# Head 2's loads and products, the q statistics and the engine orders in a convolution-attention and FFN kernel

## The chip, the cores and the metric

The kernel runs on one core of one Trainium2 chip. The metric is the device time of one execution in microseconds (us). TensorE is called PE (PEld: its weight loads), VectorE DVE, ScalarE ACT, GpSimd POOL and SyncE SP, as in the profile.

## The reference, cut to what matters

```python
def xattn(k, v, q, ssm_kernel, D, head_dim):      # k = v = ctx_2048, q = layernorm(x); (8, 128, 256)
    kv = jnp.einsum('bhil,bhjl->bijhl', k_, v_)    # 16 heads of 8 rows: all products of two rows
    y = causal convolution of kv with ssm_kernel[h] along l (by FFT of 2 * 256)
    out = y + kv * D[h]
    return jnp.einsum('bijhl,bhil->bjhl', out, q_)
def ffn(x):                                        # integer weights less 128, times a scale per row
    return down(silu(gate(x)) * up(x))             # 256 -> 704 -> 256
x = x + xattn(ctx_2048, ctx_2048, layernorm(x), ssm_kernel, D, 8)
x = x + ffn(layernorm(x))
```

All is float32. The layer norms have no weights.

## The kernel before

**Attention.** Positions (256, in two halves of 128) lie on partitions, and the work goes head by head, 16 heads. For each head `products[n]` holds the products of two of the eight context rows for all eight batches: since k = v only those with a distance of 0 to 4 rows are made, 288 columns a half are convolved. Two instructions make them: the squares (ACT, `squares(n)`) and the four other distances (POOL, `pairs(n)`); for heads 0 and 1 DVE makes all five distances at once (`all_products`, one call for each half; `DVE_MADE = 2`). The convolution is three multiplications by parts of a Toeplitz matrix of the head's taps, each run as two PE instructions: `convolve_across(n)` (first half into second) and `convolve_within(n)` (each half into itself). The Toeplitz matrices come by DMA with shifted rows, those of heads 0 to 7 from the taps as they are (`load_direct`; DVE's `direct(n)` then adds D to the diagonal), those of heads 8 to 15 from a padded copy `taps_pad` that ACT stores to device memory after POOL has added D to it (`add_skip_to_taps`). Three PSUM buffers `conv` serve the heads by the table `BUFFER`; a head may be convolved when the last head of its buffer has been read.

**q.** Two heads make a tile of 128 rows of x (`x_sb[:, t, :]`), eight tiles. For each tile DVE takes `stats_of_q` (bn_stats), `moments_of_q` (bn_aggr) and `variance_of_q` (adds eps), POOL `root_q` (power of -0.5 of one column), DVE `shift_of_q` (minus mean times root), ACT `norm_q`; PE turns the rows (`turn_q`), and ACT copies them out (`evict_q`). `multiply_terms(n)` (DVE, three instructions) multiplies a head's convolution by q. `wrap` (ACT), `merge_front`, `merge_back` and `merge_last` (POOL and DVE) add terms up for tiles 2 to 7, `sum_terms(t)` (PE) turns and sums them in PSUM, and `add_sum(t)` (DVE) adds them to x.

**FFN.** The same statistics follow for each finished tile (`stats_of_f` to `norm_f`), `turn_f` turns it, `high_f` and `low_f` split it into two 16-bit parts. Two tiles make a block. `gates(i, t)` (PE) computes a chunk of gate and up, `gate` (ACT) the silu, `hidden_units` (DVE) the product, `hidden_high` (ACT) and `low` (POOL, some on DVE) split it, `downs` (PE) multiplies by the down weights, `scale_out` and `add` finish, and SP stores.

**What sets the order.** Each engine has one list of calls written out by hand, run in that order, and semaphores carry every dependency between engines (and between dependent instructions of one engine). The loads all stand in SP's list, in one queue, but for x's tile 0, the taps and the store of `taps_pad`, which ACT issues. SP's list waits three times: for head 1's direct matrix, for those of heads 2 and 3, and for `taps_pad`'s store. PE begins with 17 matmuls on zeros.

Of the kernel before, what the change touches and what calls it, by code (L numbers as in the profile page):

```python
# [12 lines left out]
P = 128  # L13
# [26 lines left out]
DVE_MADE = 2  # L40
# [8 lines left out]
EARLY_TURNS = 6  # L49

# [24 lines left out]
def build(nc, x, ctx_skip, taps, wg_t, s_gate, wu_t, s_up, wd_t, s_down, taps_pad, out):  # L75
    with ExitStack() as ctx:
# [16 lines left out]
        minus_half = sb("minus_half", [P, 1])  # L93
# [7 lines left out]
        variance_q = sb("variance_q", [P, TILES])  # L101
        rstd_q = sb("rstd_q", [P, TILES])
# [36 lines left out]
        direct_loaded = [sem("direct0_loaded"), sem("direct1_loaded"), sem("direct2_loaded"), sem("direct4_loaded"),  # L139
# [4 lines left out]
        k_loaded = [sem("k0_loaded"), sem("k1_loaded"), sem("k2_loaded"), sem("k4_loaded"), sem("k8_loaded"), sem("k12_loaded")]  # L144
# [11 lines left out]
        q_shift = sem("q_shift")  # L156
        q_normed = sem("q_normed")
# [150 lines left out]
        def _(sp):  # L308
# [30 lines left out]
            load_k(4, 8, k_loaded[3])  # L339

            sp.wait_ge(direct_loaded[1], 16)
            load_direct(4, 6, direct_loaded[3])
            load_direct(6, 8, direct_loaded[4])
            sp.wait_ge(direct_loaded[2], 16)
            load_k(8, 12, k_loaded[4])
# [8 lines left out]
            load_k(12, H, k_loaded[5])  # L354
# [11 lines left out]
        def _(pool):  # L366
            def root_q(t):
                wait(pool, q_variance, t + 1)
                nc.gpsimd.tensor_tensor(rstd_q[:, t:t + 1], variance_q[:, t:t + 1], minus_half[:, :],  # L369
                                        ALU.pow).then_inc(q_rstd, 1)  # L370

            def root_f(t):
                wait(pool, f_variance, t + 1)
                nc.gpsimd.tensor_tensor(rstd_f[:, t:t + 1], variance_f[:, t:t + 1], minus_half[:, :],
                                        ALU.pow).then_inc(f_rstd, 1)
# [17 lines left out]
            def add(i, r):  # L393
# [9 lines left out]
                                    base=0, pattern=[[-1, P]], channel_multiplier=1).then_inc(ident_ready, 1)  # L403
            pool.wait_ge(taps_loaded, 16)
            add_skip_to_taps()
            pool.wait_ge(half_ready, 1)
# [8 lines left out]
            pool.wait_ge(k_loaded[3], 16)  # L415
            pairs(4, 0, 2)
            pairs(5, 0, 2)
            pairs(6, 0, 2)
            root_q(3)
            pairs(7, 0, 2)  # L420
            root_f(0)
            pool.wait_ge(k_loaded[4], 16)
            pairs(8, 0, 2)
            merge_front(nc.gpsimd, 2)
            root_q(4)
            pairs(9, 0, 2)
            root_f(1)
            pairs(10, 0, 2)
            root_q(5)
            pairs(11, 0, 2)  # L430
            pool.wait_ge(k_loaded[5], 16)
            pairs(12, 0, 2)
            root_q(6)
            merge_front(nc.gpsimd, 3)
            root_q(7)
            merge_front(nc.gpsimd, 4)
            low(0, 0)
            root_f(2)
            pairs(13, 0, 2)
            root_f(3)  # L440
            low(0, 1)
            low(0, 2)
            pairs(14, 0, 2)
            merge_front(nc.gpsimd, 5)
            pairs(15, 0, 2)
            merge_back(nc.gpsimd, 5)
            root_f(4)
            merge_front(nc.gpsimd, 6)
            low(0, 3)
            low(0, 4)  # L450
            merge_back(nc.gpsimd, 6)
            root_f(5)
            low(1, 0)
            low(1, 1)
            merge_front(nc.gpsimd, 7)
            low(1, 2)
            merge_back(nc.gpsimd, 7)
            root_f(6)
            add(0, 0)
            low(1, 3)  # L460
            low(1, 4)
            low(2, 0)
# [3 lines left out]
            add(0, 1)  # L466
# [11 lines left out]
        def _(act):  # L478
            def squares(n):
                nc.scalar.activation(  # L480
                    view(products[:, n:n + 1], 0, [[MADE, HALVES], [1, GROUP]]),
                    view(k_ext[:, n:n + 1], 0, [[EXT * B, HALVES], [1, GROUP]]), ACT.Square).then_inc(squares_made, 1)

# [69 lines left out]
            norm_q(1)  # L553
            wrap(0)
            evict_q(1)
            act.wait_ge(k_loaded[3], 16)
# [7 lines left out]
            act.wait_ge(k_loaded[4], 16)  # L564
# [18 lines left out]
            evict_q(5)  # L583
            act.wait_ge(scales_loaded, 3 * 16)
            gate(0, 0)
            wrap(4)
            gate(0, 1)
            hidden_high(0, 0)
            norm_q(6)
            hidden_high(0, 1)  # L590
            act.wait_ge(k_loaded[5], 16)
            squares(12)
            squares(13)
            gate(0, 2)
            evict_q(6)
            squares(14)
            hidden_high(0, 2)
            squares(15)
            gate(0, 3)
            norm_f(2)  # L600
            gate(0, 4)
            high_f(2)
            norm_f(3)
            high_f(3)
            hidden_high(0, 3)
            wrap(5)
            norm_q(7)
            gate(0, 5)
            gate(1, 0)
            evict_q(7)  # L610
            wrap(6)
            hidden_high(0, 4)
            norm_f(4)
            high_f(4)
            gate(1, 1)
            hidden_high(0, 5)
            hidden_high(1, 0)
            gate(1, 2)
            gate(1, 3)
            hidden_high(1, 1)  # L620
            wrap(7)
            norm_f(5)
            hidden_high(1, 2)
            gate(1, 4)
            high_f(5)
            gate(1, 5)
            hidden_high(1, 3)
            gate(2, 0)
            hidden_high(1, 4)
# [6 lines left out]
            hidden_high(2, 2)  # L636
            gate(2, 3)
            high_f(6)
            norm_f(7)
            gate(2, 4)  # L640
            hidden_high(2, 3)
            high_f(7)
            hidden_high(2, 4)
            gate(2, 5)
            hidden_high(2, 5)
            gate(3, 0)
            hidden_high(3, 0)
            gate(3, 1)
# [10 lines left out]
        def _(dve):  # L659
# [23 lines left out]

            def shift_of_q(t):
                wait(dve, q_rstd, t + 1)
                dve.tensor_scalar(shift_q[:, t:t + 1], moments_q[:, t, 0:1], rstd_q[:, t:t + 1], -1.0,  # L686
                                  ALU.mult, ALU.mult).then_inc(q_shift, 1)
# [93 lines left out]
            multiply_terms(0)  # L781
            variance_of_q(1)
            dve.wait_ge(direct_loaded[2], 16)
            direct(2)
            direct(3)
            dve.wait_ge(x_loaded[2], 16)
# [6 lines left out]
            dve.wait_ge(direct_loaded[3], 16)  # L793
            direct(4)
            direct(5)
            shift_of_q(2)
            moments_of_q(3)
            multiply_terms(2)
            variance_of_q(3)
            multiply_terms(3)  # L800
            add_sum(0)
            dve.wait_ge(x_loaded[3], 16)
            stats_of_q(4)
            stats_of_f(0)
            moments_of_q(4)
            dve.wait_ge(direct_loaded[4], 16)
# [402 lines left out]
```

## Time and profile before

| | |
|---|---|
| median of 3 runs | 76.82 us (76.43 to 76.84) |
| the profiled execution | 76.37 us, its span 74.6 us |
| busy, share of the span | PE 92%, DVE 83%, POOL 79%, ACT 61%, PEld 76% |
| granted TensorE clock | 1.00 |
| read from and written to device memory | 7.12 MB and 1.07 MB |

Busy times count an instruction from its start to its end; consecutive instructions of one engine overlap a little, and PE's matmuls overlap much, so a PE that is "busy" may still stand still for some tenths of a us. A stall of PE is therefore read from the distance of two starts. Line numbers are those of the kernel above.

### The profile page before, as it was taken

The page shows a single profiled execution, that of the slowest core. Times are in us where ns is not written, and L with a number is a line of the kernel's source. Part 1 is how long each engine was busy: PE and PEld are TensorE (multiplying, and loading weights), DVE is VectorE, ACT ScalarE, POOL GpSimd, SP SyncE. Part 2 cuts the span into 40 slices and gives each one's busy share as a digit, 9 for nine tenths or more (in the row PEclk, how much of TensorE's full clock was granted, in tenths as well). Part 3 has the DMA queues.
Part 4 walks back from the last instruction along what each step waited for, and adds up shares of the span by engine and source line. Part 5 has one row for each costly group of instructions (what it writes and reads, how often), then busy time and mean ns, then how long its engine had stood idle before and what let it go on. Part 6 is the DMA issues. An engine that isn't in the chain of part 4 may idle for free.

```text
span 74.6 us, 1493 instructions
## 1 busy us (share of the span) xinstructions
PE 68.8 (92%) x469; PEld 56.7 (76%) x469; DVE 62.0 (83%) x188; ACT 45.4 (61%) x115; POOL 58.6 (79%) x76
## 2 busy tenths in 40 slices
PE   4997979999999989999999999999999999999920
PEld 3754557988878848889798889797999989899810
DVE  0087899999988999999999899999968884686760
ACT  1503436460997879967746894647768796776300
POOL 6021787997999999899999999479998999339230
PEclk9999999999999999999999999999999999999999
DMA  1797998999999200000000000000002006000404
GB/s 8 194 194 225 400 291 267 370 388 399 367 355 303 78 7 0 0 0 4 9 0 0 0 0 4 0 0 0 0 13 70 0 0 211 0 9 0 141 0 141
DMA packets 7128, 8.29 MB, mean 111 GB/s; under 512 B 816, under 2 KB 6224, under 8 KB 7120
## 3 DMA queue, kind: packets, MB, share of 16 engines
q1 hardware_dynamic: 6912, 8.01, 33.8%
q10 hardware_dynamic: 208, 0.18, 0.8%
q8 instruction: 4, 0.07, 0.4%
q14 instruction: 4, 0.03, 0.1%
HBM read 7.12 MB, written 1.07 MB: 110 GB/s over the span
## 4 chain that ended last, share of the span: by engine, by line
PE 60%; POOL 17%; DVE 11%; DMA 4%; issue 3%; ACT 2%; POOLq 0%; DVEq 0%
PE conv L1016 26%; PE down L1035 13%; POOL products L385 10%; POOL rstd_q L369 4%; PE conv L983 4%; PE conv L994 4%; PE conv L992 4%; DMA x_sb<-x 4%; PE turn L963 3%; DVE terms L728 3%; PE turn L945 2%; PE turn L1035 2%; POOL terms L281 2%; DVE terms L731 1%; DVE stats_q L673 1%
## 5 line engine op out<-in xcount | busy, mean ns | idle before, releaser
L1016 PE MATMUL conv<-f_parts,wgu 128*128 128x256 f16 x176 | 22.1, 273 | 0.0
L385 POOL TENSOR_TENSOR products<-k_skip 128x512 f32<-128x512 f32 (+1 forms) x16 | 18.2, 1150 | 1.9 <-DMA k_skip<-ctx_skip 1.9
L1016 PEld LDWEIGHTS conv<-f_parts,wgu 128*128 128x128 f16 x176 | 16.6, 98 | 2.7 <-DVE hidden L743 0.3
L259 POOL TENSOR_TENSOR h_lo<-hidden,h_hi 128x256 fp32r<-128x256 f32 x18 | 13.1, 748 | 2.5 <-ACT h_hi L525 2.5
L743 DVE SCALAR_TENSOR_TENSOR hidden<-conv,su_sb,gate_act 128x256 f32<-128x256 f32 (+1 forms) x24 | 11.5, 482 | 3.0 <-ACT gate_act L520 2.7
L520 ACT ACTIVATE gate_act<-conv,sg_sb 128x256 f32<-128x256 f32 (+1 forms) x24 | 11.2, 468 | 4.1 <-PE conv L1016 3.9
L728 DVE TENSOR_TENSOR terms<-conv,q_ext 128x512 f32<-128x512 f32 x16 | 10.9, 681 | 0.4 <-PE conv L994 0.2
L992 PE MATMUL conv<-products,toeplitz 128*128 128x288 f32 x32 | 10.5, 411 | 0.5 <-DVE toeplitz L661 0.5
L983 PE MATMUL conv<-products,toeplitz 128*128 128x288 f32 x32 | 10.8, 420 | 0.1
L994 PE MATMUL conv<-products,toeplitz 128*128 128x288 f32 x32 | 10.4, 406 | 0.0
L525 ACT ACTIVATE h_hi<-hidden 128x256 fp32r<-128x256 f32 x20 | 8.3, 414 | 3.4 <-DVE hidden L743 3.1
L1035 PE MATMUL down<-wd,h_hi 128*128 128x256 f32 x35 | 9.7, 306 | 0.0
L731 DVE TENSOR_TENSOR terms<-conv,q_ext 128x384 f32<-128x384 f32 x16 | 8.8, 550 | 0.0
L1035 PE MATMUL down<-wd,h_lo 128*128 128x256 f32 x35 | 8.8, 279 | 0.0
L486 ACT ACTIVATE q_rows<-x_sb,shift_q,rstd_q 128x256 f32<-128x256 f32 x8 | 4.8, 596 | 6.2 <-DVE shift_q L686 6.2
L281 POOL TENSOR_TENSOR terms<-terms 128x512 f32<-128x512 f32 x6 | 8.4, 1398 | 0.0
L963 PE MATMUL turn<-ident,terms 128*128 128x128 f32 x60 | 7.9, 273 | 0.0
L992 PEld LDWEIGHTS conv<-products,toeplitz 128*128 128x128 f32 x32 | 5.8, 190 | 2.6 <-POOL products L385 0.9
L963 PEld LDWEIGHTS turn<-ident,terms 128*128 128x128 f32 x60 | 7.0, 141 | 0.9
L994 PEld LDWEIGHTS conv<-products,toeplitz 128*128 128x128 f32 x32 | 6.1, 190 | 1.7
L1035 PEld LDWEIGHTS down<-wd,h_hi 128*128 128x128 f32 x35 | 6.6, 189 | 0.5 <-DVE h_lo L259 0.2
L369 POOL TENSOR_TENSOR rstd_q<-variance_q,minus_half 128x1 f32<-128x1 f32 x8 | 5.3, 666 | 1.8 <-DVE variance_q L681 1.8
(65 smaller groups left out, 120.5 us busy)
## 6 DMA issues: line engine op xcount, KB each, us to landing
k_skip<-ctx_skip SPq DMA_DIRECT2D x3, 384.0 KB, 5.7
toeplitz<-taps_pad SPq DMA_DIRECT2D x2, 512.0 KB, 9.0
out<-x_sb SPq DMA_DIRECT2D x8, 128.0 KB, 1.7
toeplitz<-taps SPq DMA_DIRECT2D x3, 256.0 KB, 5.0
wg_int<-wg_t SPq DMA_DIRECT2D x1, 704.0 KB, 8.8
wu_int<-wu_t SPq DMA_DIRECT2D x1, 704.0 KB, 10.0
wd_int<-wd_t SPq DMA_DIRECT2D x1, 640.0 KB, 9.7
x_sb<-x SPq DMA_DIRECT2D x1, 512.0 KB, 6.6
```

What stands on the lines that cost most here:

```text
L259: eng.tensor_tensor(low_of(i, t), hidden[up_lanes(t), i % 2, t, :], high_of(i, t), ALU.subtract).then_inc(done, 1)
L281: eng.tensor_tensor(even, even, odd, ALU.add).then_inc(merged, 1)
L385: nc.gpsimd.tensor_tensor(view(products[:, n:n + 1], first * MADE + GROUP, [[MADE, halves], [GROUP, 4], [1, GROUP]]), view(k, 0, [[EXT * B ...
L520: nc.scalar.activation(gate_act[up_lanes(t), i % 2, t, :], gate_of(i, t), ACT.Silu, scale=sg_sb[gate_lanes(t), t:t + 1]).then_inc(gate_act ...
L728: dve.tensor_tensor(view(z, h, [[TERMS, HALVES], [P, 4], [to, GROUP]]), view(y, HALF0, [[COLS, HALVES], [GROUP, 4], [1, GROUP]]), view(q, ...
L743: dve.scalar_tensor_tensor(out=hidden[lanes, i % 2, t, :], in0=up_of(i, t), scalar=su_sb[lanes, t:t + 1], in1=gate_act[lanes, i % 2, t, :] ...
L963: done = nc.tensor.matmul(turned[:, c * P:(c + 1) * P], view(z, c * TERMS + slot, [[1, P]]), ident[:, :], is_transpose=True, start=(n == 0 ...
L983: nc.tensor.matmul(conv[BUFFER[n]][:, BANK:BANK + COLS], toeplitz[:, n, P:L], products[:, n, 0:COLS], start=True, stop=False)
L992: nc.tensor.matmul(y[:, BANK:BANK + COLS], within, products[:, n, MADE:MADE + COLS], start=False, stop=True)
L994: nc.tensor.matmul(y[:, HALF0:BANK], within, products[:, n, 0:COLS], start=True, stop=True).then_inc(conv_done, 1)
L1016: done = nc.tensor.matmul(bank_of(i, t)[:, n, :], wgu[:, c, column:column + P], f_parts[:, i % 2, part, c, :], start=(c == 0 and part == 0 ...
L1035: done = nc.tensor.matmul(down_of(i, r), part[:, r * P:(r + 1) * P], wd[:, t, :], start=own, stop=(t == FULL), skip_group_check=True)
```

## The change

- `load_k(2, 4)` and `load_direct(2, 4)` become four transfers, in the order k of head 2, matrix of head 2, k of head 3, matrix of head 3, each with a semaphore of its own.
- `DVE_MADE = 3`: head 2's products are made by DVE's `all_products(2, ..)` in two halves; `pairs(2)` and `squares(2)` go.
- The statistics of q's tiles 2 to 7 go from DVE to ACT: `center_q` gives minus the mean, `spread_of_q` the sum of squared differences, both by ACT's accumulator output. DVE makes the variance of two tiles in one instruction, POOL the root of two tiles in one. Tiles 0 and 1 keep the old way (`VECTOR_STATS = 2`).
- The lists of POOL, ACT, DVE and PE are laid out anew. The early parts stand below; later parts move single calls past one another.

```diff
-DVE_MADE = 2
+DVE_MADE = 3
+VECTOR_STATS = 2
# SP
-            load_k(2, 4, k_loaded[2])
-            load_direct(2, 4, direct_loaded[2])
+            load_k(2, 3, k_loaded[2])
+            load_direct(2, 3, direct_loaded[2])
+            load_k(3, 4, k_loaded[3])
+            load_direct(3, 4, direct_loaded[3])
             load_x(2, 4, x_loaded[2])
...
-            sp.wait_ge(direct_loaded[2], 16)
+            sp.wait_ge(direct_loaded[3], 16)
# POOL
+            def root_q_pair(t):
+                wait(pool, q_pair_variance, (t - VECTOR_STATS) // 2 + 1)
+                nc.gpsimd.tensor_tensor(rstd_q[:, t:t + 2], variance_q[:, t:t + 2], minus_half[:, :],
+                                        ALU.pow).then_inc(q_pair_rstd, 1)
...
+            root_q(0)
             add_skip_to_taps()
-            root_q(0)
-            pool.wait_ge(k_loaded[2], 16)
-            pairs(2, 0, 1)
-            pairs(2, 1, 2)
             root_q(1)
+            pool.wait_ge(k_loaded[3], 16)
             pairs(3, 0, 1)
             pairs(3, 1, 2)
-            root_q(2)
             pairs(4, 0, 2)
+            root_q_pair(2)
             pairs(5, 0, 2)
             pairs(6, 0, 2)
-            root_q(3)
             pairs(7, 0, 2)
# ACT
+            def center_q(t):
+                act.wait_ge(x_loaded[t // 2 + 1 if t < 4 else 3], 16)
+                nc.scalar.activation(scratch[:, 0, t, :], x_sb[:, t, :], ACT.Copy, scale=-1.0 / L,
+                                     accum_out=minus_mean_q[:, t:t + 1]).then_inc(q_centered, 1)
+            def spread_of_q(t):
+                wait(act, q_centered, t + 1 - VECTOR_STATS)
+                nc.scalar.activation(scratch[:, 1, t, :], x_sb[:, t, :], ACT.Square, bias=minus_mean_q[:, t:t + 1],
+                                     accum_out=spread_q[:, t:t + 1]).then_inc(q_spread, 1)
...
+            norm_q(0)
             act.wait_ge(taps_ready, 1)
             act.dma_start(taps_pad, taps_sb[:, :]).then_inc(taps_stored, 16)
-            norm_q(0)
+            act.wait_ge(k_loaded[3], 16)
+            squares(3)
             evict_q(0)
-            act.wait_ge(k_loaded[2], 16)
-            squares(2)
-            squares(3)
             norm_q(1)
+            center_q(2)
+            center_q(3)
+            spread_of_q(2)
+            spread_of_q(3)
+            squares(4)
             wrap(0)
             evict_q(1)
-            squares(4)
             norm_q(2)
             squares(5)
             squares(6)
+            squares(7)
+            evict_q(2)
+            norm_q(3)
+            center_q(4)
             wrap(1)
-            evict_q(2)
-            squares(7)
+            center_q(5)
             squares(8)
+            squares(9)
+            center_q(6)
+            spread_of_q(4)
+            spread_of_q(5)
+            spread_of_q(6)
+            evict_q(3)
+            wrap(2)
             convert_gate()
-            norm_q(3)
-            wrap(2)
-            squares(9)
-            evict_q(3)
-            norm_f(0)
-            norm_q(4)
+            center_q(7)
             convert_up()
             squares(10)
+            norm_q(4)
+            norm_f(0)
+            evict_q(4)
             high_f(0)
-            evict_q(4)
             norm_f(1)
+            spread_of_q(7)
+            high_f(1)
             squares(11)
             wrap(3)
-            high_f(1)
# DVE
+            def variance_of_q_pair(t):
+                wait(dve, q_spread, t + 2 - VECTOR_STATS)
+                dve.tensor_scalar(variance_q[:, t:t + 2], spread_q[:, t:t + 2], 1.0 / L, EPS, ALU.mult,
+                                  ALU.add).then_inc(q_pair_variance, 1)
...
             all_products(0, 0, 1)
-            moments_of_q(0)
-            all_products(0, 1, 2)
             direct(0)
+            all_products(0, 1, 2)
+            moments_of_q(0)
             variance_of_q(0)
...
             stats_of_q(1)
             moments_of_q(1)
-            multiply_terms(0)
+            all_products(2, 0, 1)
             variance_of_q(1)
             direct(2)
+            all_products(2, 1, 2)
             direct(3)
-            stats_of_q(2)
             shift_of_q(1)
-            moments_of_q(2)
+            multiply_terms(0)
             multiply_terms(1)
-            variance_of_q(2)
-            stats_of_q(3)
+            variance_of_q_pair(2)
             direct(4)
             direct(5)
+            direct(6)
             shift_of_q(2)
             multiply_terms(2)
+            shift_of_q(3)
             multiply_terms(3)
             add_sum(0)
# PE
             convolve_within(0)
+            convolve_across(1)
             turn_q(0, q_ready, 0)
-            convolve_across(1)
             convolve_within(1)
             convolve_across(2)
             convolve_within(2)
+            turn_q(1, q_ready, 1)
             convolve_across(3)
-            turn_q(1, q_ready, 1)
             convolve_within(3)
+            convolve_across(4)
             sum_terms(0, q_ready, 0)
-            convolve_across(4)
             turn_q(2, q_ready, 2)
             convolve_within(4)
             convolve_across(5)
+            turn_q(3, q_ready, 3)
             convolve_within(5)
+            convolve_across(6)
             sum_terms(1, x1_ready, 1)
-            convolve_across(6)
             convolve_within(6)
-            turn_q(3, q_ready, 3)
             convolve_across(7)
             convolve_within(7)
             sum_terms(2, x1_ready, 2)
             convolve(8)
+            turn_q(4, q_ready, 4)
             turn_f(0, x1_ready, 3)
-            turn_q(4, q_ready, 4)
             convolve(9)
             turn_f(1, f_ready, 1)
             convolve(10)
-            turn_q(5, q_ready, 5)
             gates(0, 0)
             gates(0, 1)
+            turn_q(5, q_ready, 5)
             convolve(11)
             sum_terms(3, f_ready, 2)
```

## Rows read from the trace of the kernel before

**Rows 1.** Busy time in two windows: stretch, length, engines' busy (instructions), clock, DMA.

```profile
10.50:27.00 16.50, 16.35 (x95) 13.09 (x93) 16.06 (x58) 11.28 (x30) 15.70 (x17) 1.00 0.89 296
27.00:50.00 23.00, 22.82 (x161) 19.39 (x162) 22.56 (x66) 16.31 (x43) 21.22 (x23) 1.00 0.01 1
```

**Rows 2.** Chain of waits that ended last, by engine (share of the span).

```profile
PE 60%; POOL 17%; DVE 11%; DMA 4%; issue 3%; ACT 2%; POOLq 0%; DVEq 0%
```

**Rows 3.** Timeline of PE: start, duration, line, operation, shape [idle before, releaser].

```profile
6.97 0.41 PE L937 MATMUL down<-ident,q_rows 128*128 128x128 f32 x2 [0.45 <-ACT q_rows L486]
...
8.67 0.72 PE L983 MATMUL conv<-products,toeplitz 128*128 128x288 f32 x2
9.89 0.72 PE L992 MATMUL conv<-products,toeplitz 128*128 128x288 f32 x2 [0.49 <-DVE toeplitz L661]
...
12.69 1.91 PE L963 MATMUL turn<-ident,terms 128*128 128x128 f32 x16
...
16.11 0.65 PE L983 MATMUL conv<-products,toeplitz 128*128 128x288 f32 x2
16.60 0.65 PE L992 MATMUL conv<-products,toeplitz 128*128 128x288 f32 x2
...
26.20 0.65 PE L994 MATMUL conv<-products,toeplitz 128*128 128x288 f32 x2
...
27.18 0.41 PE L945 MATMUL turn<-ident,f_rows 128*128 128x128 f32 x2 [0.33 <-DVE f_parts L714]
...
30.90 0.65 PE L983 MATMUL conv<-products,toeplitz 128*128 128x288 f32 x2
```

**Rows 4.** Groups by line and shape: count, busy us, mean ns, idle before.

```profile
L385 POOL TENSOR_TENSOR products<-k_skip 128x256 f32<-128x256 f32 x4 | 2.8, 730 | 1.9 <-DMA k_skip<-ctx_skip 1.9
L369 POOL TENSOR_TENSOR rstd_q<-variance_q,minus_half 128x1 f32<-128x1 f32 x8 | 5.3, 666 | 1.8 <-DVE variance_q L681 1.8
L486 ACT ACTIVATE q_rows<-x_sb,shift_q,rstd_q 128x256 f32<-128x256 f32 x8 | 4.8, 596 | 6.2 <-DVE shift_q L686 6.2
L525 ACT ACTIVATE h_hi<-hidden 128x256 fp32r<-128x256 f32 x20 | 8.3, 414 | 3.4 <-DVE hidden L743 3.1
L480 ACT ACTIVATE products<-k_skip 128x128 f32<-128x128 f32 x14 | 3.8, 303 | 0.0
L673 DVE BATCH_NORM_STATS2 stats_q<-x_sb 128x6 f32<-128x256 f32 x8 | 3.4, 421 | 2.6 <-DMA x_sb<-x 2.6
```

**Rows 5.** Timeline of DVE and POOL, 6 to 10 and 21 to 22 us.

```profile
6.11 0.88 DVE L667 TENSOR_TENSOR products<-k_skip 128x320 f32<-128x320 f32 x2
...
8.07 0.69 DVE L728 TENSOR_TENSOR terms<-conv,q_ext 128x512 f32<-128x512 f32 x1 [0.18 <-ACT q_ext L502]
...
9.34 0.14 DVE L681 TENSOR_SCALAR variance_q<-moments_q 128x1 f32<-128x1 f32 x1
9.40 0.61 DVE L661 SCALAR_TENSOR_TENSOR toeplitz<-anti,k_skip,toeplitz 128x128 f32<-128x128 f32 x2
...
9.56 0.59 POOL L369 TENSOR_TENSOR rstd_q<-variance_q,minus_half 128x1 f32<-128x1 f32 x1 [0.28 <-DVE variance_q L681]
...
21.49 0.66 DVE L289 TENSOR_TENSOR terms<-terms 128x512 f32<-128x512 f32 x1
...
21.52 1.04 POOL L369 TENSOR_TENSOR rstd_q<-variance_q,minus_half 128x1 f32<-128x1 f32 x1
```

**Rows 6.** Timeline of ACT, two places.

```profile
13.37 0.50 ACT L480 ACTIVATE products<-k_skip 128x128 f32<-128x128 f32 x2
...
18.80 1.38 ACT L528 ACTIVATE wgu<-wg_int 128x1408 f16<-128x1408 int32 x1 [1.99 <-DMA wg_int<-wg_t]
```

**Rows 7.** Timeline of DMA issues on ACT's and SP's queues.

```profile
4.53 0.36 ACTq L547 DMA_DIRECT2D taps_pad<-taps_sb  x1
...
8.55 0.34 SPq L320 DMA_DIRECT2D k_skip<-ctx_skip  x1
...
9.46 0.47 SPq L315 DMA_DIRECT2D toeplitz<-taps_pad  x1
```

More of the change, by code:

```diff
@@ L446, in _ @@
             merge_back(nc.gpsimd, 5)
+            low(0, 3)
             root_f(4)
             merge_front(nc.gpsimd, 6)
-            low(0, 3)
+            merge_back(nc.gpsimd, 6)
             low(0, 4)
-            merge_back(nc.gpsimd, 6)
             root_f(5)
@@ L454, in _ @@
             low(1, 1)
+            low(1, 2)
             merge_front(nc.gpsimd, 7)
-            low(1, 2)
             merge_back(nc.gpsimd, 7)
-            root_f(6)
             add(0, 0)
@@ L581, in _ @@
+            squares(12)
             norm_q(5)
             convert_down()
-            evict_q(5)
             act.wait_ge(scales_loaded, 3 * 16)
             gate(0, 0)
+            gate(0, 1)
             wrap(4)
-            gate(0, 1)
             hidden_high(0, 0)
+            evict_q(5)
             norm_q(6)
+            norm_q(7)
+            gate(0, 2)
             hidden_high(0, 1)
-            act.wait_ge(k_loaded[5], 16)
-            squares(12)
+            gate(0, 3)
+            evict_q(6)
@@ L593, in _ @@
+            hidden_high(0, 2)
             squares(13)
-            gate(0, 2)
-            evict_q(6)
+            norm_f(2)
+            norm_f(3)
             squares(14)
-            hidden_high(0, 2)
+            high_f(2)
+            hidden_high(0, 3)
+            gate(0, 4)
             squares(15)
[L599 to L603, printed above, removed]
             high_f(3)
-            hidden_high(0, 3)
+            gate(0, 5)
@@ L606, in _ @@
             wrap(5)
-            norm_q(7)
-            gate(0, 5)
+            hidden_high(0, 4)
+            evict_q(7)
+            hidden_high(0, 5)
             gate(1, 0)
-            evict_q(7)
+            hidden_high(1, 0)
             wrap(6)
-            hidden_high(0, 4)
             norm_f(4)
+            gate(1, 1)
+            gate(1, 2)
+            hidden_high(1, 1)
             high_f(4)
[L615 to L618, printed above, removed]
+            hidden_high(1, 2)
@@ L639, in _ @@
             norm_f(7)
+            hidden_high(2, 2)
             gate(2, 4)
+            high_f(7)
             hidden_high(2, 3)
-            high_f(7)
+            gate(2, 5)
             hidden_high(2, 4)
-            gate(2, 5)
+            gate(3, 0)
+            gate(3, 1)
             hidden_high(2, 5)
-            gate(3, 0)
             hidden_high(3, 0)
-            gate(3, 1)
             gate(3, 2)
@@ L827, in _ @@
             add_sum(2)
-            stats_of_q(7)
+            multiply_terms(7)
             shift_of_f(1)
-            moments_of_q(7)
-            variance_of_q(5)
+            shift_of_q(5)
             stats_of_f(2)
-            multiply_terms(7)
             low_f(0)
-            shift_of_q(5)
-            variance_of_q(6)
             multiply_terms(8)
+            variance_of_q_pair(6)
             low_f(1)
+            moments_of_f(2)
             merge_back(dve, 3)
             multiply_terms(9)
-            variance_of_q(7)
@@ L842, in _ @@
             merge_last(dve, 3)
-            merge_back(dve, 4)
+            shift_of_q(6)
             dve.wait_ge(scales_loaded, 3 * 16)
             hidden_units(0, 0)
-            shift_of_q(6)
+            shift_of_q(7)
             hidden_units(0, 1)
-            moments_of_f(2)
+            variance_of_f(2)
+            merge_back(dve, 4)
             add_sum(3)
-            variance_of_f(2)
+            multiply_terms(10)
             stats_of_f(3)
-            multiply_terms(10)
+            merge_last(dve, 4)
@@ L866, in _ @@
             low_f(3)
+            hidden_units(0, 4)
+            hidden_units(0, 5)
             moments_of_f(4)
-            shift_of_q(7)
+            multiply_terms(13)
             variance_of_f(4)
-            multiply_terms(13)
             merge_last(dve, 5)
+            hidden_units(1, 0)
+            low(0, 5)
             shift_of_f(4)
-            hidden_units(0, 5)
-            hidden_units(1, 0)
+            multiply_terms(14)
             add_sum(5)
-            multiply_terms(14)
+            hidden_units(1, 1)
@@ L978, in convolve_across @@
                 if n < DIRECT:
-                    pe.wait_ge(direct_loaded[n if n < 2 else n // 2 + 1], 16)
+                    pe.wait_ge(direct_loaded[n if n < 4 else n // 2 + 2], 16)
                 else:
```

162 lines of the change are left out of this document (79 added, 83 removed).

## The prediction

> **What bounds the kernel now.** I read the windows first, then the chain of waits, then TensorE's starts in the timeline. TensorE (PE) is busy 22.82 of 23.00 us between 27 and 50 us, and VectorE (DVE) 22.56 of them; between 10.5 and 27 us PE is busy 16.35 of 16.50 [rows 1]. The chain gives PE 60% of the span, and POOL and DVE, on its early part, 28% [rows 2]. A matmul's busy time hides short stalls, so holes are looked for in the starts [rows 3]. A head's six convolution matmuls start 0.243 apart (two of them from 16.11 to 16.60; 1.46 for a head), and the sixteen transposes of sum_terms(0) 0.109, so two take 0.22. From 12.69 to 26.20 every start follows at these steps. The holes are early: 0.45 and a slow start before turn_q(0) at 6.97 (waits for q's normalised rows), 0.73 between conv_across(2) at 8.67 and conv_within(2) at 9.89 (0.49 of the 1.22 are its own two matmuls), and 0.5 before turn_f(1) at 27.18, which waits for DVE. After 30.90 there is none above 0.25. So at most about 2 us are to be had, all before 27.2, and whatever PE gains there it keeps, if the others follow; DVE, 98% busy behind it, is the one to fear.
>
> **The loads.** Four transfers in place of two, with the same bytes, in one queue. SP waited for the direct matrices of heads 2 and 3 and went on at 8.55 [rows 7], so they landed just before; head 2's half of them comes no later. Were nothing earlier, direct(2), now at 8.50, would wait 0.05. Two more issues (of some 0.4 each, by the issue at 8.55 [rows 7]) stand ahead of loads that follow, but SP then waits for direct_loaded[1] as before: nothing.
>
> **Up to the end of head 1: nothing.** direct(0) goes ahead of the second half of head 0's products, so the moments of tile 0 are taken last and its variance, POOL's root and shift_of_q(0), for which DVE stands still, come about 0.20 later (an estimate: a moments instruction and its end, which variance waits for). Head 1's products, behind that shift, start at 6.31 (6.11 before [rows 5]); the first half is ready at 6.75 and conv_across(1) starts at 6.88, ahead of turn_q(0), which was ready at 7.2 (the hole stays, in another place). turn_q(0) at 7.44, conv_within(1) 7.66 to 8.63, against 8.67.
>
> **Head 2: -0.53, then -0.61.** DVE: direct(1) 7.11, stats(1) 7.45, moments 7.91, first half of products(2) 8.04 to 8.51 (two halves cost 0.88 [rows 5]), variance(1), direct(2) 8.50 (0.31 by the pair at 9.40, [rows 5]), second half 8.76 to 9.24. Head 2's second part starts at 9.35 for 9.89, and PE leaves head 2 at 10.40 for 10.93. POOL makes no pairs for head 2 (two of 0.73 [rows 4]); it does root_q(1) 8.71 to 9.27 and has pairs(3) at 10.0 and 10.7. ACT waits for head 3's load, squares(3), then evict_q(0), now done at about 9.0 (1 us later; DVE asks for it at 9.5), norm_q(1) 9.63 to 10.23. turn_q(1) 10.40, head 3 10.62 to 12.08; the same work ended at 12.69 [rows 3]: 0.61.
>
> **Head 4 gives 0.36 of it back.** conv_across(4) now stands ahead of sum_terms(0). It needs head 1's PSUM buffer, so multiply_terms(1): terms(0) starts at 9.53 behind the products (8.07 before; 1.27 each, 8.07 to 9.34 [rows 5]) and terms(1) ends at 12.15. It needs squares(4), which stand on ACT behind center_q(2), (3) and spread_of_q(2), (3). No row shows an activation with an accumulator. A Copy of 256 columns takes 0.414, with two per-partition operands 0.596 [rows 4]; a Square with one is put between, 0.50. Consecutive ones overlap by about 0.10 (two squares of 0.303 in 0.50, [rows 4, 6]). The reading of the accumulator is the unknown, r: none at the low end, 0.27 at the high end (nearly a whole one of the shortest activations, 0.303, without overlap). From 128 and 256 columns one of no columns would be 0.19, an estimate, and 0.10 with the overlap, the row nearest to it: r = 0.10. So centers step 0.41, spreads 0.50: from 10.14, squares(4) 11.96 to 12.27, conv_across(4) 12.37 with a slow first matmul to 12.93, sum_terms(0) to 14.67, turn_q(2) (its root is one POOL instruction for two tiles, ready in time), head 4 done at 15.86 for 16.11 [rows 3]. Gain 0.25.
>
> **From there to 30 us: +0.55.** Heads 5 to 8, sum_terms(1) and (2) find everything there (pairs(5) to (8) done at 14.4, 15.7, 16.9, 18.2; wraps and merges before PE asks), so conv(8) starts 0.25 earlier, at 23.07. ACT: norm_q(3) 15.50, then three centers, three spreads, wraps, squares, convert_gate 20.27, center(7), convert_up 21.96, norm_q(4) 23.53, norm_f(0) 24.04 to 24.64. turn_q(4) at 24.53 waits for nothing; turn_f(0) at 24.78 just so: no slack. DVE without the statistics reaches low_f(0) when high_f(0) is ready, ends it at 26.2, and turn_f(1) at 26.46 doesn't wait. That removes the 0.5 and a slow start: conv(11) at 30.10 for 30.90, 0.80.
>
> **POOL against DVE: -0.35 of that.** At 21.52 POOL's root of one column took 1.04 beside a DVE merge with two SBUF inputs (21.49, 0.66), where its mean is 0.666 and the one at 9.56, beside direct(2) and (3), took 0.59 [rows 4 to 6]. Head 2's products on DVE also have two SBUF inputs, and root_q(1) starts at 8.71 among them: it costs between 0 and 0.47 (held to the end of the second half). I take the upper end, for the merge is nearer in size than the direct. shift_of_q(1), terms(0) and terms(1), norm_q(1) and all behind it shift by 0.35, and conv_across(4) with them. [...]
>
> **Beside the path.** POOL loses two half pairs (1.46) and three of eight roots (2.0); DVE loses six bn_stats (0.42 each) with their aggregations, some 3 us net of head 2's products (0.88); ACT gains about 6.7 (six times 0.41 + 0.50 + 0.20), all before 27 us. After 30 us the orders change, but PE finds its inputs: DVE is 0.8 ahead at hidden(0,0) and loses that lead by turn_f(2) near 37 us, where a gain over 0.5 would be cut. The gain stays 0.45.
>
> **Sum.** 0.61 - 0.36 + 0.55 - 0.35 = 0.45. The profiled execution took 76.37 (span 74.6 and 1.8 around it); it becomes 75.92. The median of the runs, 76.82, lies 0.45 above that execution, so the time is 76.82 - 0.45 = 76.4. Within 0.5% is within 0.38 us, about what a measurement here can tell.
>
> **Rivals.** (1) POOL is not held up: 0.80, cut to 0.7 to 0.8 near 37 us, and 1.2 with r near 0: 75.6 to 76.1. For it: the 0.59 at 9.56 [rows 5]. Against: the 1.04. (2) ACT becomes the bound, slower. Place: turn_q(4) and turn_f(0) at 24.5, which wait for norm_q(4) and norm_f(0) behind twelve new activations. Four readings stand before squares(4), seven between norm_q(3) and norm_q(4). With r = 0.20 squares(4) come 0.4 later, norm_f(0) another 0.7, with no slack: 1.1 lost, 0.65 slower than before, 77.5; with r = 0.27, 78.2. It decides from r = 0.14 on, where 0.04 times 11 eats the 0.45. Against it: ACT's overlaps in every row [rows 6]. (3) The loads come later: no change. taps_pad was stored at 4.53, and SP issued the first padded load at 9.46, just when that had landed. Now the store stands behind norm_q(0), at 6.5, and SP goes on at about 11.4. If the queue's backlog does not hide it, the gate weights, which ACT waited for until 18.80 [rows 6, 7], come at 20.7, where convert_gate wants them at 20.27: 0.45 lost, 76.8. Against: those weights, issued next after 9.46, took nine us to land, so the queue holds work for longer than 1.9 us.
>
> **Chances.** Forecast 0.38 (76.1 to 76.7; 0.22 of it faster by over 0.5%, 0.16 within). Rival 1: 0.20, faster. Rival 2: 0.27, slower. Rival 3 and what else eats the gain: 0.15, of it 0.10 within and 0.05 slower. Faster 0.42, same 0.26, slower 0.32. The range goes from rival 1's low end to rival 2 at r = 0.20: 75.6 to 77.6.
>
> **What would show it.** Right: conv_within(2) at 9.3 to 9.5, head 3 done by 12.1 to 12.4, no wait of PE at turn_f(1), conv(11) 0.4 to 0.8 earlier. ACT's step from one center to the next is 0.31 + r: over 0.46 is rival 2, seen as PE waiting at turn_q(4) or turn_f(0). root_q(1) of 0.56 is rival 1, of 0.9 or more the forecast. An ACT wait before convert_gate is rival 3. Wrong altogether: PE stalls after 30 us, which I found no reason for.

## The result: slower, 77.66 us for the 76.4 forecast

The changed kernel took 77.66 us (median of 4 runs, 77.08 to 77.78), the kernel before 76.83 beside it: a ratio of 1.012, 95% interval 1.008 to 1.016. It is slower by 0.83, where I had forecast 0.45 faster. (Ratios leave disturbed runs out, so a ratio can differ a little from the quotient of two medians.) The profiled execution took 77.08, the shortest of the four, with a span of 75.3.

The windows and, last, the chain by engine of the kernel after, for [rows 1, 2]; columns as there:

```profile
10.50:27.00 16.50, 16.21 (x96) 13.42 (x96) 16.02 (x48) 15.10 (x51) 15.78 (x15) 1.00 0.90 305
27.00:50.00 23.00, 22.00 (x152) 18.16 (x152) 22.62 (x63) 17.34 (x46) 20.18 (x21) 1.00 0.00 1
...
PE 63%; DVE 23%; DMA 4%; issue 3%; POOL 1%; ACT 1%; SPq 0%; DVEq 0%; POOLq 0%
```

POOL leaves the chain (17% to 1%), as the change would have it, and DVE takes its place (11% to 23%). PE loses 0.82 us of busy time between 27 and 50 us, where I had found no reason for a stall. Its starts in the timeline of the kernel after, for [rows 3]:

```profile
8.91 0.65 PE L1013 MATMUL conv<-products,toeplitz 128*128 128x288 f32 x2
9.42 0.75 PE L1022 MATMUL conv<-products,toeplitz 128*128 128x288 f32 x2
...
10.50 0.38 PE L967 MATMUL down<-ident,q_rows 128*128 128x128 f32 x2
11.17 0.72 PE L1013 MATMUL conv<-products,toeplitz 128*128 128x288 f32 x2 [0.29 <-DVE terms L778]
...
12.70 0.65 PE L1013 MATMUL conv<-products,toeplitz 128*128 128x288 f32 x2
...
16.12 0.65 PE L1013 MATMUL conv<-products,toeplitz 128*128 128x288 f32 x2
...
26.68 0.38 PE L975 MATMUL turn<-ident,f_rows 128*128 128x128 f32 x2
...
30.37 0.65 PE L1013 MATMUL conv<-products,toeplitz 128*128 128x288 f32 x2
...
47.48 0.41 PE L975 MATMUL turn<-ident,f_rows 128*128 128x128 f32 x2 [0.97 <-DVE x_sb L735]
```

Head 3 ends at 12.70 and head 4 at 16.12, as before (12.69, 16.11): the early part gained nothing. turn_f(1) at 26.68 no longer waits, and conv(11) starts at 30.37 for 30.90: 0.53 gained there. Then one hole of 0.97 before turn_f(4) at 47.48. DVE and POOL about it, and about the early part (timeline of the kernel after, for [rows 5]):

```profile
8.79 0.59 POOL L381 TENSOR_TENSOR rstd_q<-variance_q,minus_half 128x1 f32<-128x1 f32 x1 [2.24 <-DVE variance_q L714]
9.29 0.34 DVE L694 SCALAR_TENSOR_TENSOR toeplitz<-anti,k_skip,toeplitz 128x128 f32<-128x128 f32 x1
9.35 2.89 POOL L402 TENSOR_TENSOR products<-k_skip 128x256 f32<-128x256 f32 x3
...
10.75 0.28 DVE L778 TENSOR_TENSOR terms<-conv,q_ext 128x128 f32<-128x128 f32 x1
...
43.94 1.27 POOL L291 TENSOR_TENSOR terms<-terms 128x512 f32<-128x512 f32 x1
43.99 1.51 DVE L269 TENSOR_TENSOR h_tail<-hidden,h_tail 64x256 fp32r<-64x256 f32 x1
45.66 0.68 DVE L771 TENSOR_TENSOR terms<-conv,q_ext 128x512 f32<-128x512 f32 x1
46.92 0.41 DVE L735 TENSOR_TENSOR x_sb<-x_sb,turn 128x256 f32<-128x256 f32 x1
```

The row to look at is low(0, 5), DVE's subtraction for h_tail: 1.51 us for 64x256 elements. It starts 0.05 after POOL's merge_front(6) (43.94, 1.27) and ends 0.29 after it. The same instruction in the kernel before, which the new order moved, from its timeline of DVE and POOL:

```profile
43.03 0.68 DVE L298 TENSOR_TENSOR terms<-terms 128x512 f32<-128x512 f32 x1
43.19 1.66 POOL L281 TENSOR_TENSOR terms<-terms 128x512 f32<-128x512 f32 x1
...
48.30 0.42 DVE L259 TENSOR_TENSOR h_tail<-hidden,h_tail 64x256 fp32r<-64x256 f32 x1
```

At 48.30 POOL was idle and low(0, 5) took 0.42. The difference is 1.09. And merge_front(6) met another DVE instruction with two SBUF inputs even then (43.03), started second, and took 1.66: the same event with the roles exchanged, at no cost that shows: PE has no stall over 0.1 from there to 50.3.

### The profile page after: what moved, and what is told of

Same layout as the page of the kernel before. It is cut to its first block, busy times and chain, and to the rows that moved or that the text cites. A ratio compares the mean times of both kernels' runs of the same rounds, so it can differ in the third digit from the quotient of the medians.

```text
span 75.3 us, 1500 instructions
## 1 busy us (share of the span) xinstructions
PE 69.2 (92%) x469; PEld 57.3 (76%) x469; DVE 62.1 (82%) x175; ACT 50.8 (68%) x138; POOL 56.9 (76%) x71
## 4 chain that ended last, share of the span: by engine, by line
PE 63%; DVE 23%; DMA 4%; issue 3%; POOL 1%; ACT 1%; SPq 0%; DVEq 0%; POOLq 0%
PE conv L1046 20%; PE down L1065 9%; PE turn L993 8%; PE conv L1013 8%; PE conv L1022 7%; PE conv L1024 7%; DMA toeplitz<-taps 4%; DVE terms L771 4%; DVE terms L774 3%; DVE hidden L786 3%; DVE products L700 3%; PE turn L975 2%; DVE toeplitz L694 2%; DVE terms L778 1%; PE down L967 1%
## 5 line engine op out<-in xcount | busy, mean ns | idle before, releaser
L402 POOL TENSOR_TENSOR products<-k_skip 128x512 f32<-128x512 f32 (+1 forms) x14 | 16.7, 1210 | 0.1
L269 POOL TENSOR_TENSOR h_lo<-hidden,h_hi 128x256 fp32r<-128x256 f32 x18 | 14.4, 809 | 2.7 <-ACT h_hi L547 2.7
L1024 PEld LDWEIGHTS conv<-products,toeplitz 128*128 128x128 f32 x32 | 6.1, 190 | 1.7
L1013 PEld LDWEIGHTS conv<-products,toeplitz 128*128 128x128 f32 x32 | 5.3, 193 | 2.3 <-DVE products L700 0.9
L1022 PEld LDWEIGHTS conv<-products,toeplitz 128*128 128x128 f32 x32 | 5.6, 190 | 1.8 <-DVE products L700 0.7
```

Of the source, the lines that this page charges most:

```text
L269: eng.tensor_tensor(low_of(i, t), hidden[up_lanes(t), i % 2, t, :], high_of(i, t), ALU.subtract).then_inc(done, 1)
L402: nc.gpsimd.tensor_tensor(view(products[:, n:n + 1], first * MADE + GROUP, [[MADE, halves], [GROUP, 4], [1, GROUP]]), view(k, 0, [[EXT * B ...
L1013: nc.tensor.matmul(conv[BUFFER[n]][:, BANK:BANK + COLS], toeplitz[:, n, P:L], products[:, n, 0:COLS], start=True, stop=False)
L1022: nc.tensor.matmul(y[:, BANK:BANK + COLS], within, products[:, n, MADE:MADE + COLS], start=False, stop=True)
L1024: nc.tensor.matmul(y[:, HALF0:BANK], within, products[:, n, 0:COLS], start=True, stop=True).then_inc(conv_done, 1)
```

## The experiments

The theory, **A**: a VectorE and a POOL instruction, both with two SBUF operands, exclude each other, and the second to start stands until the first ends; low(0, 5) and merge_front(6) are such a pair, and what stands behind low(0, 5) on DVE (shift_of_f(4), multiply_terms(14), add_sum(5)) makes turn_f(4) late. The main rival, **B**: add_sum(5) was put too late in DVE's order in any case, or the new orders after 30 us are worse as a whole.

**e1: low(0, 5) moved back, behind hidden_units(1, 1).**

```diff
-            low(0, 5)
             shift_of_f(4)
             multiply_terms(14)
             add_sum(5)
             hidden_units(1, 1)
+            low(0, 5)
```

> The changed kernel with one call moved: VectorE's low(0, 5) goes from ahead of shift_of_f(4) to behind hidden_units(1, 1). In the changed kernel's trace it starts at 43.99, 0.05 after POOL's merge_front(6), takes 1.51 where its like takes 0.42, and PE then stands still 0.97 before turn_f(4). Theory A (the two exclude each other, both reading two tiles of SBUF, and VectorE came second): add_sum(5) ends about 1.4 earlier, PE waits under 0.3 at turn_f(4), the time falls by 0.7 to 1.1 against the changed kernel, to 0.995 to 1.003 of the kernel before. Theory B (the place in the order alone: low and terms(14) ahead of add_sum(5), no exclusion): only low's own 0.42 comes off, PE still waits 0.5, time falls by 0.4, ratio about 1.006.

Measured: 77.21, ratio 1.007 (1.003 to 1.011). Timeline of POOL, DVE and PE in e1:

```profile
9.16 1.59 POOL L402 TENSOR_TENSOR products<-k_skip 128x256 f32<-128x256 f32 x2
9.35 0.80 DVE L694 SCALAR_TENSOR_TENSOR toeplitz<-anti,k_skip,toeplitz 128x128 f32<-128x128 f32 x1
...
46.86 0.38 PE L975 MATMUL turn<-ident,f_rows 128*128 128x128 f32 x2
...
46.93 0.72 POOL L269 TENSOR_TENSOR h_lo<-hidden,h_hi 128x256 fp32r<-128x256 f32 x1
47.21 0.73 DVE L269 TENSOR_TENSOR h_tail<-hidden,h_tail 64x256 fp32r<-64x256 f32 x1
...
50.39 0.63 PE L993 MATMUL turn<-ident,terms 128*128 128x128 f32 x4 [0.35 <-DVE f_parts L757]
```

turn_f(4) no longer waits, as A had it, but low(0, 5) meets POOL's low(0, 4) and takes 0.73, and PE waits a little later. The time missed A's range and is the one that B gave (1.006), so e1 alone does not decide between them. A second pair shows early: direct(3), 0.34 in the kernel after, took 0.80 because pairs(3, 0, 1) started first.

**e2: POOL waits for low(0, 5) before merge_front(6)**, the order of DVE left alone.

```diff
             root_f(4)
+            pool.wait_ge(tail_ready, 1)
             merge_front(nc.gpsimd, 6)
```

> The changed kernel with one wait added: POOL starts merge_front(6) only when VectorE's low(0, 5) is done. Theory A: low(0, 5) takes 0.42 to 0.5 at 43.99, POOL's merge_front(6) starts near 44.5 for 43.94, PE's wait at turn_f(4) shrinks from 0.97 to under 0.2, time falls 0.6 to 1.0 against the changed kernel. Theory B: low keeps its 1.5, and nothing is gained (POOL's 1 us of delay may even cost).

Measured: **76.26, ratio 0.996 (0.993 to 0.9995)**. Timeline of DVE, POOL and PE in e2:

```profile
43.94 0.42 DVE L269 TENSOR_TENSOR h_tail<-hidden,h_tail 64x256 fp32r<-64x256 f32 x1
44.44 1.28 POOL L291 TENSOR_TENSOR terms<-terms 128x512 f32<-128x512 f32 x1 [0.52 <-DVE h_tail L269]
...
45.78 0.41 DVE L736 TENSOR_TENSOR x_sb<-x_sb,turn 128x256 f32<-128x256 f32 x1
46.34 0.41 PE L976 MATMUL turn<-ident,f_rows 128*128 128x128 f32 x2
```

A wait *added* to an engine makes the kernel faster than before. add_sum(5) starts 1.14 earlier than in the kernel after, turn_f(4) doesn't wait. DVE's order is the same and B had nothing to gain here, so the place of add_sum(5) alone is not the cause.

**e3: add_sum(5) ahead of multiply_terms(14)**, rival B's cure.

```diff
-            multiply_terms(14)
             add_sum(5)
+            multiply_terms(14)
```

> The changed kernel with add_sum(5) ahead of multiply_terms(14) on VectorE. Theory A: low(0, 5) still takes 1.5, but add_sum(5), for which PE waits, ends 1.27 earlier, near 46.1; then norm_f(4) of ACT (done at 46.4) ends the wait, near 46.5: PE waits 0.2 to 0.3, time falls by 0.5 to 0.8. Theory B: the same 0.8. It tells how much of the price hangs on the order behind the held instruction.

Measured: 77.49, ratio 1.014 (1.007 to 1.020). low(0, 5) still took 1.52; turn_f(4) is in time, but PE waits 0.37 before sum_terms(6), for DVE's low_f(4), and 0.23 before turn_f(5), for add_sum(6). The gain of 0.5 to 0.8 that both theories gave did not come: the delay of DVE comes out elsewhere.

**e4: the orders of the kernel before after some 31 us**, behind the new early part.

```diff
 ... (each engine: the new list up to about 31 us)
-            (the new list from there on)
+            (the list of the kernel before from there on)
```

> The changed kernel up to about 31 us (loads, head 2 on VectorE, statistics on ACT, early orders), and from sum_terms(3), merge_back(4), hidden_high(0, 1) and root_f(2) on the four lists as they stood in the kernel before. In the changed kernel's trace conv(11) starts 0.53 earlier than before, as forecast near 0.45; if the whole loss is in the late orders, this one keeps 0.3 to 0.5: 0.993 to 0.997 of the kernel before. If the early part itself costs something later (ACT or VectorE late), it stays at 1.00 or above.

Measured: 77.24, ratio 1.008 (1.004 to 1.011), and unclear: in its profile direct(3) took 0.82, and PE waits 0.40 before gates(0, 2) and 0.32 before turn_q(6). That execution took 77.90, 0.66 above the median. Perhaps the old late lists don't fit the new early ones, which is not shown. It says nothing on A against B.

**e5 and e6: a wait for the early pair.** e5 is e2, e6 the kernel after, both with pairs(3, 0, 1) held until direct(3) is done.

```diff
             pool.wait_ge(k_loaded[3], 16)
+            pool.wait_ge(direct_ready, 4)
             pairs(3, 0, 1)
```

> The changed kernel with two waits of POOL: merge_front(6) after low(0,5), and pairs(3,0,1) after direct(3). Theory A (each of the two places is a pair of VectorE and POOL instructions with two SBUF inputs, of which the second to start is held for all of the first): direct(3) takes 0.34 every time, terms(0) starts by 9.75, low(0,5) takes 0.42; the runs gather at the fast end of e2's 75.89 to 76.77, so a median of 75.9 to 76.1 and a ratio to the kernel before of 0.990 to 0.994. Rival (the spread of e2's runs has another source, and the early pair costs nothing that lasts): the same as e2, 0.996 and the same spread. If the wait itself delays head 3 (pairs(3,1,2) later than terms(0)'s end at 11.03), worse than e2.

> The changed kernel with the early wait alone (pairs(3,0,1) after direct(3)). Theory A: the late pair still costs (low(0,5) 1.5, a hole of about 1.0 at turn_f(4)), the early one does not: the runs gather at the lowest of the changed kernel's, 77.1, a ratio of 1.003 to 1.007. Rival: 1.012 as without the wait, spread as before.

Measured on one chip: e5 **76.19, ratio 0.994 (0.992 to 0.996)**; e6 77.28, 1.009 (1.006 to 1.012). They differ by the late wait alone, and by 1.09 us (some 0.3 either way by their intervals): as much as low(0, 5) loses (1.51 less 0.42). The early wait does less than I expected, both forecasts are missed: e5 lies within e2's interval, e6 within that of the kernel after. What it leaves is seen in e5 (timeline of DVE):

```profile
9.03 0.35 DVE L696 SCALAR_TENSOR_TENSOR toeplitz<-anti,k_skip,toeplitz 128x128 f32<-128x128 f32 x1 [0.49 <-DMA toeplitz<-taps]
...
10.19 0.69 DVE L773 TENSOR_TENSOR terms<-conv,q_ext 128x512 f32<-128x512 f32 x1
```

direct(2) waits for its matrix (by 0.59 in e3's profile, not at all in that of the kernel after), so terms(0) starts at 10.19 for 9.68. (e5's profiled execution, 76.50, lies 0.31 above its median.)

**e7: the loads of heads 2 and 3 joined again**, in e5.

```diff
-            load_k(2, 3, k_loaded[2])
-            load_direct(2, 3, direct_loaded[2])
-            load_k(3, 4, k_loaded[3])
-            load_direct(3, 4, direct_loaded[3])
+            load_k(2, 4, k_loaded[2])
+            load_direct(2, 4, direct_loaded[2])
...
```

> e5 with the loads of heads 2 and 3 joined again into one transfer each (k, then the direct matrices), so the separate transfers alone are undone. My prediction's step gave the loads nothing. If the joined matrices land at 8.5 as in the kernel before, it equals e5 within 0.002. If they land when the second of the separate ones does (9.15), direct(2) waits about 0.5 and the second half of head 2's products, direct(3), terms(0) and head 3 come about 0.4 to 0.5 later: a ratio 0.005 to 0.007 above e5's.

Measured: 76.34, ratio 0.997 (0.994 to 0.999). direct(2) waits 0.39 for its matrix, no more than e5's 0.49. The two come out 0.15 apart by the medians, 0.2 by the ratios, and the intervals overlap; these runs can't tell more of what the separate transfers are worth.

**e8: head 2's products back on POOL and ACT**, in e5 without the early wait.

```diff
-DVE_MADE = 3
+DVE_MADE = 2
...
+            pairs(2, 0, 1)
+            pairs(2, 1, 2)
             root_q(1)
...
-            all_products(2, 1, 2)
```

> e5 with head 2's products back on POOL (two half pairs before root_q(1)) and ACT (squares(2)), without the early wait, whose place pairs(3) then passes anyway. Theory (head 3 is released by multiply_terms(0), not by head 2's end, so head 2's products on VectorE gain nothing by themselves): conv_within(2) 9.4 to 9.9, conv_across(3) still at 11.2 to 11.4, the ratio within 0.003 of e5. Rival, the step of the prediction (head 2 on VectorE is worth 0.53 to 0.61): 0.5 to 0.6 us above e5, a ratio of 0.998 or more. Direct(2) may be held beside pairs(2,1,2), which would show as 0.6 or more in place of 0.34.

Measured: 76.22, ratio 0.997 (0.994 to 0.9996), where the rival asked for 0.5 more than e5's 76.19. The medians are 0.03 apart; the interval takes in the rival's least ratio, 0.998, so 0.2 to 0.3 is not excluded. Timeline of e8:

```profile
8.41 1.11 DVE L700 SCALAR_TENSOR_TENSOR toeplitz<-anti,k_skip,toeplitz 128x128 f32<-128x128 f32 x2
...
11.33 0.72 PE L1016 MATMUL conv<-products,toeplitz 128*128 128x288 f32 x2 [0.28 <-DVE terms L784]
```

Two directs took 1.11 beside POOL's pairs (0.61 in [rows 5]), and still conv_across(3) starts at 11.33, for 11.17 in the kernel after, waiting for terms(0) in both. Head 2's products on VectorE are worth nothing that these runs can tell, and not the 0.53 to 0.61.

**e9 and e11: head 3 earlier.** e9 is e5 with evict_q(0) ahead of squares(3) on ACT and the second half of head 2's products ahead of direct(2); e11 is e9 with terms(0) ahead of direct(3), the early wait moved to pairs(4). The edit of e11 on DVE:

```diff
+            all_products(2, 1, 2)
             dve.wait_ge(direct_loaded[2], 16)
             direct(2)
-            all_products(2, 1, 2)
-            dve.wait_ge(direct_loaded[3], 16)
-            direct(3)
             shift_of_q(1)
             multiply_terms(0)
+            dve.wait_ge(direct_loaded[3], 16)
+            direct(3)
```

> e5 with what waits for late loads put behind what doesn't: on VectorE the second half of head 2's products ahead of direct(2), on ACT evict_q(0) ahead of squares(3). Theory (head 3 is released by multiply_terms(0), and that was late in e5's profile, 10.19, because direct(2) stood 0.49 for its matrix with the products behind it, and because evict_q(0) stood behind squares(3) and the load of head 3's k): terms(0) starts at 9.7 to 9.8 and conv_across(3) by 11.25 with the matrix as late as in e5, so 0.3 to 0.45 better than e5 where the matrix is late and equal where it is early: a ratio of 0.989 to 0.993, and less spread. Rival (what comes out there is lost again later, as ACT's chain to norm_f(0) has no slack): the ratio stays at e5's 0.994.

> e9 with shift_q(1) and multiply_terms(0) ahead of direct(3), and POOL's early wait moved from pairs(3) to pairs(4), so that direct(3) is not held. It gives the step of my prediction that failed what it lacked: head 3's PSUM buffer earlier. Theory: terms(0) ends at about 10.6 to 10.75, conv_across(3) starts at 10.8 to 10.9 behind turn_q(1), head 3 is done 0.3 earlier than in e9; of that conv_across(4), which then waits for squares(4), gives back 0 to 0.3. Ratio 0.986 to 0.992, or e9's where squares(4) give it all back. Rival: direct(3), now after terms(0), is late for conv_within(3), or terms(0) beside pairs(3) is held, and it is slower than e9.

Measured: e9 76.22, ratio 0.994 (0.991 to 0.997); e11 76.23, 0.9945 (0.992 to 0.997). PE's timeline, e9 and then e11:

```profile
11.21 0.72 PE L1015 MATMUL conv<-products,toeplitz 128*128 128x288 f32 x2 [0.22 <-DVE terms L780]
...
12.74 0.65 PE L1015 MATMUL conv<-products,toeplitz 128*128 128x288 f32 x2
```

```profile
10.93 0.72 PE L1015 MATMUL conv<-products,toeplitz 128*128 128x288 f32 x2 [0.22 <-DVE terms L780]
...
12.55 0.75 PE L1015 MATMUL conv<-products,toeplitz 128*128 128x288 f32 x2
```

Both did to head 3 what they were to do (terms(0) at 9.72 and 9.44, conv_across(3) at 11.21 and 10.93), and both came out at e5's time. Of e11's 0.28 at conv_across(3), 0.19 is left at conv_across(4), 0.08 at turn_q(2) (14.97 and 14.89; 14.93 in the kernel after) and the same 0.08 at conv(11) (30.40 and 30.32), and none in the median. So it is lost again by turn_q(2). e9 misses its number, and its rival (lost again later) stands; e11 ends at e9's time, which it had allowed for.

**e10: the merge cut in two**, in e6, with no late wait.

```diff
+        def merge_front_by_halves(eng, t):
...
+            for h in range(HALVES):
...
+                done = eng.tensor_tensor(even, even, odd, ALU.add)
+            done.then_inc(merged, 1)
...
-            merge_front(nc.gpsimd, 6)
+            merge_front_by_halves(nc.gpsimd, 6)
```

> e6 (the changed kernel with the early wait) with POOL's merge_front(6) cut into two instructions of half its width, and no wait ahead of them. Theory A (an instruction that starts second is held until the first one ends): low(0,5) is held for one half only, some 0.65 to 0.75, so it takes 0.9 to 1.1 in place of 1.51; the hole before turn_f(4) of 1.1 to 1.25 shrinks by 0.4 to 0.6, the ratio to the kernel before goes from e6's 1.0087 to 1.001 to 1.004. Rival (the two share the port and each is slowed by the other's traffic): low(0,5) stays near 1.5, or is lengthened in proportion, and the time stays.

Measured: 76.65, ratio 1.001 (0.998 to 1.004), for e6's 1.009. Timelines of POOL, DVE and PE, e6 and then e10:

```profile
44.37 1.28 POOL L291 TENSOR_TENSOR terms<-terms 128x512 f32<-128x512 f32 x1
44.42 1.51 DVE L269 TENSOR_TENSOR h_tail<-hidden,h_tail 64x256 fp32r<-64x256 f32 x1
...
47.91 0.41 PE L976 MATMUL turn<-ident,f_rows 128*128 128x128 f32 x2 [0.98 <-DVE x_sb L736]
```

```profile
44.00 1.60 POOL L299 TENSOR_TENSOR terms<-terms 128x256 f32<-128x256 f32 x2
44.05 0.97 DVE L269 TENSOR_TENSOR h_tail<-hidden,h_tail 64x256 fp32r<-64x256 f32 x1
...
47.00 0.41 PE L985 MATMUL turn<-ident,f_rows 128*128 128x128 f32 x2 [0.43 <-DVE x_sb L745]
```

This settles the form of A for this pair. low(0, 5) drops by 0.54, to 0.97: it gets through after the first half (0.73), and now POOL's second half waits for it (0.91). The hole shrinks by 0.55, the time by 0.6 (0.0079 of 76.6). Had the two merely slowed each other by their traffic, cutting the merge, with the same bytes, would not have let low(0, 5) through in the middle.

The rows give a price too, which I had not worked out. The second instruction loses what is left of the first one when it starts, less 0.13 to 0.14 in these rows (less 0.19 for direct(3) in e1), in either direction:

- DVE behind POOL: 1.22 left, 1.09 lost (43.99, kernel after); 0.68 left, 0.55 lost (44.05, e10).
- POOL behind DVE: 0.52 left, 0.39 lost (43.19, kernel before); 0.63 left, 0.49 lost (the root at 21.52, [rows 5], which takes 0.55 unheld); 0.17 left, 0.04 lost (the root at 8.79, kernel after).

A does not hold for every such pair: three directs beside a root of two columns took 0.34 each, though two of them started behind it. The rows, the first from the kernel before, the others from the kernel after:

```profile
11.94 0.55 POOL L369 TENSOR_TENSOR rstd_q<-variance_q,minus_half 128x1 f32<-128x1 f32 x1 [0.40 <-DVE variance_q L681]
...
8.62 0.34 DVE L694 SCALAR_TENSOR_TENSOR toeplitz<-anti,k_skip,toeplitz 128x128 f32<-128x128 f32 x1
...
12.28 0.87 DVE L694 SCALAR_TENSOR_TENSOR toeplitz<-anti,k_skip,toeplitz 128x128 f32<-128x128 f32 x3
...
12.46 0.73 POOL L386 TENSOR_TENSOR rstd_q<-variance_q,minus_half 128x2 f32<-128x2 f32 x1 [0.21 <-DVE variance_q L719]
```

## Why the prediction was wrong

**The step that failed** is "After 30 us the orders change, but PE finds its inputs ... The gain stays 0.45." At 30 us the profiled gain stood at 0.53. Then 1.09 went in one instruction that the new order had put beside a POOL merge. With that pair apart and nothing else changed (e2), the time is 76.26, and 76.19 in e5: 0.36 and 0.41 below the kernel before beside them, near the 0.45 forecast. The e6-e5 pair shows the 1.09 by itself, e10 its form. The profiled executions (77.08 and 76.37) differ by 0.71, and the distances of PE's starts add up to 0.73. Behind conv(11) the kernel after stalls 0.19 before sum_terms(5), 1.14 before turn_f(4) and 0.25 near 70.6, the kernel before 0.18 near 50.6 and 0.14 near 69.9: 1.26 more, less the 0.53 gained. The stalls of 0.19 and 0.25 stand in e2 too (0.20, 0.23), so they don't come from low(0, 5); I did not test them.

I had the mechanism in hand and priced it in one place and one direction: POOL's root held by DVE, -0.35, at root_q(1). There it did not come (0.59, [rows 5] had the same), so the condition of rival 1 was met, and its time (75.6 to 76.1) was off all the same. I took the 1.04 at 21.52 and the 0.59 at 9.56 for a matter of the neighbour's size. By the price above it is what was left of the neighbour, 0.63 and 0.18, and the trace of the kernel before showed it. The Trainium skill, "SBUF — State Buffer", section "Who interferes with whom", says that a VectorE instruction with two SBUF inputs contends with a GpSimd one that reads SBUF, and that the order of issue decides which of them blocks. The trace agrees: the held one was POOL at 43.19 in the kernel before (1.66), DVE at 43.99 in the kernel after (1.51); by the section's words the two directs that started behind the root at 12.46 would contend with it too, and they lost nothing: there the measurement decides. My sum had the contention with POOL as the one held, and not that a new order can turn it round.

**Up to head 1:** forecast nothing; conv_across(2) at 8.91 for 8.67, so 0.24 later.

**Head 2:** its second part at 9.42 (forecast 9.35) and turn_q(1) at 10.50 (10.40) were right. The 0.61 at head 3's end was not: 12.70. I had missed that head 3 takes head 0's PSUM buffer, so waits for multiply_terms(0), which my own working moved from 8.07 to 9.53. BUFFER and heads_until stand in the code; I applied them to head 4 and not to head 3. e8 agrees from the other side.

**Head 4:** the 0.36 to be given back was not there to give. The accumulator's size was right (timeline of ACT, kernel after, for [rows 6]):

```profile
10.30 0.40 ACT L498 ACTIVATE scratch<-x_sb 128x256 f32<-128x256 f32 x1
10.60 0.19 ACT L498 ACTIVATION_READ_ACCUMULATOR scratch<-x_sb 128x1 f32 x1
...
11.09 0.49 ACT L503 ACTIVATE scratch<-x_sb,minus_mean_q 128x256 f32<-128x256 f32 x1
...
20.45 1.37 ACT L550 ACTIVATE wgu<-wg_int 128x1408 f16<-128x1408 int32 x1
...
24.17 0.59 ACT L513 ACTIVATE f_rows<-x_sb,shift_f,rstd_f 128x256 f32<-128x256 f32 x1
```

Centers step 0.40 (10.30, 10.70) and spreads 0.50 (11.09, 11.59), for 0.41 and 0.50 forecast. turn_q(4) and turn_f(0) don't wait, so rival 2 (ACT the bound) is out, though its time, 77.5, came nearest. SP issued the first padded load at 11.07 for 9.46, as rival 3 had it, but convert_gate at 20.45 starts with no wait on the gate weights: its price is out too.

**To 30 us:** +0.55 forecast, 0.53 measured, at the place named (turn_f(1)). So the sum at 30 us (0.45 against 0.53) was right by luck, by errors that cancelled: 0.61, -0.36 and -0.35 were all about nothing.

**Open:** the profiled execution is the shortest of its four, and the median lies 0.58 above it. direct(3) held by pairs(3, 0, 1) (e1, e3, e4: about 0.8 for 0.34) and a late matrix for direct(2) (0.32 to 0.59 in e3 to e7) would make such a difference, but no trace of those runs exists, and e9, which removes both, gained nothing on e5.

## What to carry to other kernels

When an edit moves a VectorE instruction with two SBUF inputs, read what POOL does at its new place, and price both directions of the collision with what is left of the *other* engine's instruction at the start of the second one: 0.05 us of order decided here whether 1.1 us fell on an engine with time to spare or on the one that feeds TensorE. A busy row well above its like (1.66 for 1.27 on POOL) is the warning, even where it costs nothing yet. One semaphore wait on the engine that had time fixed it here (e2).

## What the runs showed that I had not expected

An activation with an accumulator leaves a second instruction, ACTIVATION_READ_ACCUMULATOR, of 0.19, of which 0.09 to 0.10 is left in the step. The duration of a held instruction contains its standing time (1.51), and shows as busy, not as a wait: DVE was 22.62 of 23.00 us busy, and no view shown here put the lost 1.09 down to POOL. The load for direct(2) made DVE wait 0.49 in e5's profiled execution and not at all in that of the kernel after, which has the same loads; in e9's, PE stood 0.92 before conv_across(1) for head 1's matrix.
